# Query's exchanged half for a rotary product: from a third projection on TensorE to four DMAs over partitions

## The reference, cut to what matters

```python
q = sh(xn @ Wq.T + bq); k = sh(xn @ Wk.T + bk); v = sh(xn @ Wv.T + bv)
scores = jnp.einsum('bhqd,bhkd->bhqk', q, k)
r = _pos_emb(S)                                   # [sin | cos], 4 + 4 columns
rel = jnp.einsum('bhqd,ld->bhql', q + u[None, :, None, :], r)
scores = (scores + _rel_shift(rel, S, S)) * HEAD_DIM ** (-0.5)
```

## Time and profile before

| what | value |
|---|---|
| time, median of 3 runs | 2714.39 us (2713.71 to 2714.42) |
| the profiled execution's own time | 2718.72 us |
| its span, first to last instruction | 2716.9 us |
| mean granted TensorE clock | 0.984 |
| busy share PE, PEld, DVE, ACT, POOL | 94%, 77%, 76%, 68%, 42% |

### The profile page before, as it was taken

One profiled execution on the slowest core, in us unless ns is written; L12 is line 12 of the kernel. 1 busy time (PEld: TensorE's weight loads), 2 busy tenths in 40 slices (PEclk: granted clock), 3 DMA queues, 4 the chain that ended last, 5 costly groups with the idle time before them and its releaser, 6 DMA issues. The chain is left out here.

```text
span 2716.9 us, 81211 instructions
## 1 busy us (share of the span) xinstructions
PE 2554.8 (94%) x31744; PEld 2083.5 (77%) x31744; DVE 2077.3 (76%) x5069; ACT 1853.1 (68%) x2837; POOL 1138.7 (42%) x2072
## 2 busy tenths in 40 slices
PE   0699999999999999999999999999999999598898
PEld 0478888888888888888888888888888887476676
DVE  6588888888888888888888888878888886377774
ACT  1277777777777777777777777777777777454454
POOL 3344444444444444444444444444444443133332
PEclk9699999999999999999999999999999999799999
DMA  4222222222222222222222222222222221100000
GB/s 125 71 73 73 74 78 73 73 74 73 67 71 69 74 73 73 73 74 73 73 73 73 71 69 69 72 74 73 74 73 73 74 70 42 35 25 27 23 20 16
DMA packets 194970, 179.18 MB, mean 66 GB/s; under 512 B 20656, under 2 KB 190256, under 8 KB 194608
## 3 DMA queue, kind: packets, MB, share of 16 engines
q1 hardware_dynamic: 194608, 174.19, 23.6%
HBM read 14.73 MB, written 4.19 MB: 7 GB/s over the span
## 5 line engine op out<-in xcount | busy, mean ns | idle before, releaser
L586 ACT ACTIVATE probs<-bank 128x1024 f32<-128x1024 f32 x768 | 787.0, 1025 | 501.1 <-PE bank L457 501.1
L754 DVE TENSOR_REDUCE rowmax<-bank 128x4 f32<-128x1024 f32 (+1 forms) x768 | 936.3, 1219 | 214.7 <-PE bank L421 214.4
L457 PE MATMUL bank<-qstack,kstack 64*128 64x256 f32 (+1 forms) x4096 | 438.1, 313 | 0.0
L421 PE MATMUL bank<-kstack,qstack 62*128 62x128 f32 (+1 forms) x4096 | 413.0, 300 | 0.0
L887 POOL TENSOR_TENSOR rotated<-turn_s,turn_c 128x256 f32<-128x256 f32 x128 | 93.8, 733 | 615.2 <-DVE turn_s L729 615.2
L625 ACT ACT_TABLE_LOAD x256 | 328.4, 1283 | 4.5
L421 PEld LDWEIGHTS bank<-kstack,qstack 62*128 62x128 f32 x4096 | 291.4, 189 | 37.1 <-issue 1.1
L457 PEld LDWEIGHTS bank<-qstack,kstack 64*128 64x128 f32 x4096 | 309.8, 188 | 9.6
L415 PE MATMUL bank<-mask_half,eye_half 64*128 64x256 bf16 (+2 forms) x3072 | 303.2, 276 | 12.3 <-DVE rowmax L754 11.7
L452 PE MATMUL bank<-maskT_half,eye_half 64*128 64x256 bf16 (+2 forms) x3072 | 303.0, 276 | 1.8 <-ACT probs L586 1.8
L847 POOL TENSOR_SCALAR ve<-mv 128x2 f32<-128x2 f32 x256 | 56.7, 221 | 566.1 <-DVE mv L698 565.5
(11 more groups left out here) (144 smaller groups left out, 5435.5 us busy)
## 6 DMA issues: line engine op xcount, KB each, us to landing
qstack<-base SPq DMA_DIRECT2D x768, 128.0 KB, 2.5
kstack<-base SPq DMA_DIRECT2D x384, 128.0 KB, 2.5
qstack<-maxrows SPq DMA_DIRECT2D x256, 16.0 KB
xin<-in_x SPq DMA_DIRECT2D x16, 256.0 KB, 2.9
out<-ot SPq DMA_DIRECT2D x16, 256.0 KB, 2.4
w_qkv<-in_w_qkv SPq DMA_DIRECT2D x1, 1024.0 KB, 8.5
w<-in_w SPq DMA_DIRECT2D x4, 256.0 KB, 2.7
w_in<-in_w_in SPq DMA_DIRECT2D x1, 768.0 KB, 5.9
```

Source lines behind the costliest of these rows:

```text
L421: last = pe.matmul(bank[:, b, i * wide:(i + 1) * wide], qstack[rows, r, p0 + i, t * 128:(t + 1) * 128], kstack[rows, r, p0 + i, 0:wide], s ...
L457: last = pe.matmul(bank[:, 2 + b, i * wide:(i + 1) * wide], kstack[rows, r, p0 + i, kt * 128:(kt + 1) * 128], qstack[rows, r, p0 + i, q0:S ...
L586: act.activation(probs[:, (ROUNDS * n + k) % PR], bank[:, 2:4, :], ACT.Exp, scale=SCALE).then_inc(exp_done, 1)
L754: dve.tensor_reduce(rowmax[:, t, :, p0:p0 + heads], bank[:, 0:2, :].rearrange("p b (h c) -> p b h c", h=heads), AX_X, ALU.max).then_inc(ma ...
```

## The change

The third projection goes. `turn_c` is now taken from bank 5 (query itself) with the signs of the cosines exchanged, four DMAs over partitions carry it into a new tile `turn_x` in the order of the other half, and POOL adds `turn_s` and `turn_x`. Weights and biases lose the columns of the third projection. In the lists, both products stand in round 1 on DVE, the cosines' first; `turned` stands in round 2 on POOL behind `v_padded`; and SP issues the exchange ahead of `content`.

```diff
+            def exchange(n):
+
+                sp.wait_ge(turn_steps, 2 * n + 1)
+                at_least(sp, rot_ready, n)
+                for c in range(4):
+                    o = 32 * (c ^ 1)
+                    sp.dma_start(turn_x[32 * c:32 * c + 32], turn_c[o:o + 32]).then_inc(turn_landed, 16)
...
                 if live(s):
+                    exchange(s)
                     content(s)
...
-                    product_of_parts(pe, bank[:, b, 0:S], w(2), x)
...
             def turn_q(n, half):
 
-                if half == 0:
-                    dve.wait_ge(qk_first, n + 1)
+                dve.wait_ge(qk_first, n + 1)
+                if half == 1:
+                    at_least(dve, turn_landed, 64 * n)
                 else:
-                    dve.wait_ge(qkv_done, 2 * (n + 1))
-                at_least(dve, rot_ready, n)
-                dve.scalar_tensor_tensor((turn_s, turn_c)[half][:], bank[:, 5 + half, 0:S],
-                                         b_cols[:, layer(n), 2 + half:3 + half], turn[:, half], ALU.add, ALU.mult
+                    at_least(dve, rot_ready, n)
+                dve.scalar_tensor_tensor((turn_s, turn_c)[half][:], bank[:, 5, 0:S],
+                                         b_cols[:, layer(n), 2:3], turn[:, half], ALU.add, ALU.mult
                                          ).then_inc(turn_steps, 1)
 
             def v_out(n):
+                dve.wait_ge(qkv_done, 2 * (n + 1))
...
                     if k == 0 and live(s):
-                        turn_q(s, 1)
                         v_out(s)
...
                     if k == 1 and live(s):
+                        turn_q(s, 1)
                         turn_q(s, 0)
                         split_rest(s)
...
             def turned(n):
                 pool.wait_ge(turn_steps, 2 * (n + 1))
+                pool.wait_ge(turn_landed, 64 * (n + 1))
                 at_least(pool, rot_rest, n)
-                pool.tensor_tensor(rotated[:], turn_s[:], turn_c[:], ALU.add).then_inc(rot_ready, 1)
+                pool.tensor_tensor(rotated[:], turn_s[:], turn_x[:], ALU.add).then_inc(rot_ready, 1)
...
-                    if k == 1 and live(s):
-                        turned(s)
                     if k == 1 and live(s - 5):
                         add_row(s - 5, b_2, xn2_ready, 2 * (s - 4), b2_added)
...
                     if k == 2 and live(s - 2):
                         v_padded(s - 2)
+                    if k == 2 and live(s):
+                        turned(s)
```

More of the change, by code:

```diff
@@ L120, in position_tables @@
     whole = (TILES, HD, PLACES, S)
-    s8, c8 = np.concatenate([sin, sin], axis=1).T, np.concatenate([cos, -cos], axis=1).T
+    s8, c8 = np.concatenate([sin, sin], axis=1).T, np.concatenate([-cos, cos], axis=1).T
     turn = np.stack([np.broadcast_to(s8[None][per], whole).reshape(128, S),
@@ L152, in layers_program @@
         bank = ctx.enter_context(nc.psum_tensor("bank", [128, 8, 512], F32))
-        w_qkv = sb("w_qkv", [128, LAYERS, 4 * D])
-        w_now = sb("w_now", [128, 2, 2, 3 * D], F32R)
+        w_qkv = sb("w_qkv", [128, LAYERS, 3 * D])
+        w_now = sb("w_now", [128, 2, 2, 2 * D], F32R)
         w_o = sb("w_o", [128, LAYERS, D])
@@ L164, in layers_program @@
         ln_cols = sb("ln_cols", [128, LAYERS, 4])
-        b_cols = sb("b_cols", [128, LAYERS, 4])
-        u_cols = sb("u_cols", [128, LAYERS, 2])
+        b_cols = sb("b_cols", [128, LAYERS, 3])
+        u_cols = sb("u_cols", [128, LAYERS, 1])
         b_1 = sb("b_1", [128, LAYERS, FC])
@@ L190, in layers_program @@
         turn_c = sb("turn_c", [128, S])
+        turn_x = sb("turn_x", [128, S])
         rotated = sb("rotated", [128, S])
@@ L252, in layers_program @@
         turn_steps = sem("turn_steps")
+        turn_landed = sem("turn_landed")
         rot_ready = sem("rot_ready")
@@ L395, in f2 @@
                     at_least(pe, h2_ready, n - 6)
-                    product_of_parts(pe, bank[:, b, 0:S], w(2), x)
                     for t in range(T):
                         last = pe.matmul(bank[:, b, S + t * D:S + (t + 1) * D], xn1T[:, t * 128:(t + 1) * 128],
-                                         w_qkv[:, layer(n), 3 * D:4 * D], start=True, stop=True)
+                                         w_qkv[:, layer(n), 2 * D:3 * D], start=True, stop=True)
                     last.then_inc(qkv_done, 1)
@@ L796, in _ @@
             dve.wait_ge(consts_landed, 16 * CONST_DMAS)
-            dve.tensor_tensor(b_cols[:, :, 2:4], b_cols[:, :, 2:4], u_cols[:], ALU.add).then_inc(consts_cast, 1)
+            dve.tensor_tensor(b_cols[:, :, 2:3], b_cols[:, :, 2:3], u_cols[:], ALU.add).then_inc(consts_cast, 1)
             dve.wait_ge(consts_cast, 4)
@@ L853, in split_qkv @@
                 at_least(pool, qkv_done, 2 * B * (ly - 1))
-                w, high = w_qkv[:, ly, 0:3 * D], w_now[:, ly % 2, 0]
+                w, high = w_qkv[:, ly, 0:2 * D], w_now[:, ly % 2, 0]
                 pool.tensor_copy(high, w).then_inc(weights_high, 1)
@@ L1380 @@
     feature = (heads[:, None, :] * HD + np.arange(HD)[None, :, None]).reshape(D)
-    other = (heads[:, None, :] * HD + (np.arange(HD)[None, :, None] + HD // 2) % HD).reshape(D)
     wq, bq, u = i("L0_attn_Wq"), i("L0_attn_bq"), i("L0_attn_u_bias").reshape(LAYERS, D)
@@ L1385 @@
         "x": i("L0_attn_x"),
-        "w_qkv": np.concatenate([wq[:, feature], i("L0_attn_Wk")[:, feature], wq[:, other], i("L0_attn_Wv")],
+        "w_qkv": np.concatenate([wq[:, feature], i("L0_attn_Wk")[:, feature], i("L0_attn_Wv")],
                                 axis=1).transpose(0, 2, 1),
-        "b_cols": np.stack([bq[:, feature], i("L0_attn_bk")[:, feature], bq[:, feature], bq[:, other]], axis=1).reshape(LAYERS * 4, D).T,
-        "u_cols": np.stack([u[:, feature], u[:, other]], axis=1).reshape(LAYERS * 2, D).T,
+        "b_cols": np.stack([bq[:, feature], i("L0_attn_bk")[:, feature], bq[:, feature]], axis=1).reshape(LAYERS * 3, D).T,
+        "u_cols": u[:, feature].T,
         "b_v": i("L0_attn_bv"),
```

## The result

| | median | ratio to before | 95% interval |
|---|---|---|---|
| before | 2714.05 us | 1 | |
| changed | 2791.51 us (2790.37 to 2795.45) | 1.0289 | 1.0271 to 1.0307 |

The change makes the kernel slower by 77 us. The direction was forecast, but the forecast size, 35 us (2749), is less than half of it; the measured time lies near the upper end of the range (2798). The profiled execution took 2790.37 us with a span of 2788.6, 71.7 us more than before.

What follows compares the result with a forecast made beforehand. PE was taken to set the pace, with POOL's slack only 1.56 us. Slots 0.24 us longer over 124 slots gave 30 us, the first slots 5: 2714.4 + 35 = 2749 us, range 2700 to 2798.

Steps and rivals of the forecast that it cites:

- PE's part: On PE, the third product's three matmuls go: 0.37 us less per slot, 47 us over 127 slots on PE alone.
- the forecast floor: Exchange at 2.99 us leaves PE the bound again: -46 + 5 us, 2673 us; chance 0.03.
- The chain: From DVE's `turn_c` through SP's exchange and POOL to PE: PE waits 0.6 us, each slot 0.24 us longer.
- the distance between issues: On SP's queue, exchange DMAs issued 0.55 us apart (ends 0.47 and 0.62): 1.65 us to the fourth issue.
- The landing: Fourth exchange DMA lands 1.95 us after issue (ends 1.8 and 2.5); POOL starts 0.08 us behind it.
- The first slots: At the start, with little work to cover the exchange, units 0 and 1 come late: 5 us, counted once.
- What was costed at nothing: SP's queue with 3.8 us to spare before `maxima`, stack products two slots later, narrower weights and splits: 0 us.
- The quick exchange: Rival: issues and landing take 3.21 us, slot -0.15 us, -13 us in all, 2701 us; chance 0.2.
- the case that cancels: Rival: exchange takes 3.27 to 3.36 us, time within 0.2% (5.4 us) of before; chance 0.12.
- The slow landing: Rival: issues 0.62 us, landing 2.5 us, together 4.36 us; +0.76 us a slot, 2813 us; chance of over 4.0 us 0.12.
- The lower clock: Rival: PE's 0.6 us standstill per slot lowers its granted clock; chance 0.03 together with late maxima, priced like the slow landing.
- The rule against splitting one transfer over partitions: Skill page on DMA: splitting over disjoint partitions brings nothing, one transfer of 128 partitions is better; cited against the change.

Runs made afterwards that it cites:

- the runs with `turned` later, with and without the projection: Changed kernel with POOL's `turned(s)` moved behind `xn1_split(s + 1)`: 2672.07 us; the same with a third product of parts put back on PE: 2718.13 us.
- The run by columns: Changed kernel, each of the four DMAs carrying 64 columns of all 128 partitions to the same partitions, nothing exchanged between partitions: 2786.31 us.
- the run without the wait: Changed kernel, POOL adding `turn_s` and `turn_c` without waiting for the four exchange DMAs, which are still issued: 2672.78 us.
- the run with eight DMAs: Changed kernel with the same exchange in eight DMAs of 16 partitions instead of four of 32: 3386.91 us.

## Why the prediction was right in its way and wrong in its size

**PE's part** was right. The three matmuls were counted at 0.37 us; the runs with `turned` later, with and without the projection, lie 46 us apart, 0.36 over 127 slots. PE alone gives the forecast floor: 2673 us was written, 2672.1 was measured where the wait is away.

**The chain** was right in its order and in all links but one. The trace of the changed kernel, 120 steady slots, means:

| link | forecast, us | measured, us |
|---|---|---|
| PE's projection to `turn_c`'s start | 8.37 | 8.33 |
| `turn_c` itself | 0.48 | 0.48 |
| release of SP | 0.03 | 0.03 |
| first to fourth issue | 1.65 | 2.06 |
| fourth issue to `rotated` | 2.03 | 2.00 |
| `rotated` to the low part's end | 4.98 | 4.99 |
| release of PE | 0.05 | 0.05 |
| sum, one slot | 17.59 | 17.94 |

(the first row of the forecast is the old distance less the 0.74 us by which `turn_c` comes before the old `turn_s`). The forecast slot was 0.24 us longer than before; the measured one is 0.55 us longer, as the mean of all 127. By the prediction's own terms the exchange took 3.98 us (2.06 + 2.00, less POOL's 0.08), still inside its bracket of 3.36 to 4.0 us, at the upper end.

**The step that failed** is a term of the sum, "the distance between issues", of which the prediction said "I take 0.55, with 0.47 and 0.62 as ends". It measured 0.69 in the mean, outside of its own ends: 0.60 us to the second issue, 0.71 and 0.74 to the third and fourth. Two things were wrong in it.

- The 0.55 was drawn between the small DMAs of this queue and the plain loads. The run by columns shows that the loads were the wrong kin: with either shape the exchange's issues take 0.59 to 0.60 us in the median, and 0.58 to 0.65 us from start to start. The nearest row of before was that of `base`, 0.62 apart. In the median the fourth issue starts 1.87 us behind the first: 0.22 us of the miss.
- Some issues take 1 to 2 us. The median of a row hides them, and they add the other 0.19 us: 34 of the 120 slots have one among the exchange's first three. The prediction had no term for them. This stood in the trace of the kernel before, in the view of tile `base` (whole span, min/median/max in ns), which the prediction didn't read:

```profile
L344 SPq DMA_DIRECT2D qstack<-base x384: 532/598/1769, 79.3 to 2272.1; - x192
L346 SPq DMA_DIRECT2D kstack<-base x384: 558/603/1991, 80.0 to 2272.7; - x192
```

Before, SP stood idle 4.6 us in a slot ahead of `content` and 4.1 us ahead of `maxima` (589.0 and 527.7 us over the span), which took up a long issue. The change put four issues on the path, and each delay went through to PE.

The 0.41 us, over 124 slots, are some 51 us; the other links together came out 0.06 us shorter, which takes some 7 us back. That is, within 2 us, the distance from the forecast's 35 us to 77. The two parts weigh differently. In the middle slot the wider spacing is nearly made up for by the other links: it takes 17.67 us, 0.09 over the forecast's 17.58. The 120 slots together lie 27 us above 120 middle slots, and 22 us of that are between the first and the fourth issue. So more than half of the miss of 42 us is the long issues.

**The landing** was right in its sum: the fourth DMA lands 1.87 us behind its issue in the mean (1.84 in the median) and POOL starts 0.13 us later, 2.00 together, forecast 1.95 and 0.08.

**The first slots** were right: 5 us forecast, 4.2 measured ahead of the first maxima. `rotated` of the first unit came 3.1 us later (forecast 2.6) and that of the second 4.6 (forecast 6.2).

**What was costed at nothing** stayed at nothing: SP was in time for the maxima (it waited for line 782 in all 128 slots, 436.1 us), and the run without the wait shows that issues and traffic by themselves cost no time.

**The rivals.** The quick exchange is out: the shortest issue of the 512 took 0.55 us, and two never started closer than 0.59 us. With it go the floor and the case that cancels. The slow landing is out too. Its price was added up wrongly: 4.36 us against the 3.60 of the forecast is 0.76 us over the forecast's slot and so 1.00 us over the slot of before, which makes 129 us and 2843, not 2813. The lower clock played hardly a part here. PE's wait is 0.5 to 0.8 us in most slots, and the granted clock fell to 0.5 for four stretches of 3.4 us in the four layers; but the run with eight DMAs, with a wait of 3.45 us in the slot shown, has it. The rule against splitting one transfer over partitions (the Trainium skill, "DMA: Bandwidth & Descriptors", section "Rules for kernel authors") agrees with the runs in what it advises. The page reasons with the DMA engines that both parts share; in the trace the price stands on SP's queue, 0.69 us for each further issue, and eight DMAs for the same bytes took 4.75 us from the first to the last issue where four took 2.06. No run carries the exchange in one transfer, so what that would give is open.

**The cure** was in the prediction's own sentence on what is queued behind the waiting instruction. The exchange isn't needed soon; the low part of the next unit is. With the two in that order on POOL the change brings what PE's list promised: 2672.1 us, 1.4% less than before.

## What to carry to other kernels

When a product on the busiest engine is traded for transfers, ask first which engine will wait for the landing and what stands behind that wait in its list; move the wait behind the work that others need. Here that alone turned a loss of 77 us into a gain of 41. Cost a DMA on the path by issue and landing apart, with the mean of the issue times of the same kind of DMA on the same queue, and look at the maximum of the row as well as at its median. Idle time of an engine hides added work only if the work stands ahead of the wait, not behind it.

## What the runs showed of the hardware

**Long issues meet packets of the instruction queue.** The page of the changed kernel lists the DMA queues with their packets, MB and share:

```profile
q1 hardware_dynamic: 219184, 190.73, 25.4%
q8 instruction: 244, 4.00, 0.6%
```

The 244 packets of the second queue carry 16 KB each and last 1.1 us in the median. Laid over SP's issues between 140 and 2300 us, packet records against issue records:

```
issues                      count   those that overlap a packet of q8
changed kernel, over 0.8 us    82      82
changed kernel, under 0.7 us 1720     107
before, over 0.8 us            68      68
before, under 0.7 us         1286      98
```

In these two kernels every long issue lies over such a packet, and of the short ones 6 to 8% do (20 more, between 0.7 and 0.8 us, stand in no row). That the packet holds the issue up is the plain reading; no run here took the packets away, so it is not shown. With two issuing engines it is not the only way to a long issue: SP's second issue, at 0.84 us, is there without a packet.

**The clock after a wait.** In the run with eight DMAs PE waits 3.5 us in the mean, and behind that wait the granted clock stood at 0.5 for a while in 118 of 120 steady slots. The changed kernel's common waits of 0.5 to 0.8 us left it at 1.00, as in this steady slot:

```profile
1218.00:1222.00 4.00, 3.49 (x40) 2.92 (x44) 2.12 (x8) 3.63 (x8) 1.45 (x3) 1.00 0.40 115
```

Its four falls to 0.5, 3.4 us each, stand behind waits of 1.4 to 1.9 us; other waits as long had none.

**Two issuing engines.** Issues from ACT and SP at the same moment overlap. The first of each takes 0.51 and 0.56 us, the second 0.61 and 0.84, where from one queue the first takes 0.56 and the others 0.59.
